# Four chained image blocks on one core: attention on 32-row tiles of TensorE in two sets of four banks, and a token-major third residual and tail

## What is computed

```
L0: x1 = x + wp.attention(q, k, v of groupnorm(x))                   one head, 256 x 256 scores
L1: pam = x1 + g1 * attention(16-channel q, k; 128-channel v)
    x2  = pam + g2 * softmax(max - pam.pam^T).pam                    attention between channels
L2: q, k = [x2 ; emb] @ Wq, Wk (8 heads of 16),  v = x2 @ Wv
    x3  = x2 + Wout.concat_h softmax(q_h.k_h^T / 4).v_h + bout       16 score matrices of 256 x 256 in all
L3: f = chan_ln(x3);  q, k, v = depthwise3x3(conv1x1(f))
    q = softmax over each head's 16 channels, k = softmax over the pixels
    o = silu(q.(k^T v));   x4 = x3 + chan_ln(out_w.o)
    out = x4 + ff_w2.chan_ln(gelu(ff_w1.chan_ln(x4)))
```

## Time and profile before

| | |
|---|---|
| median of 3 runs | 92.72 us (92.59 to 92.74) |
| the profiled execution | 93.64 us, of which the span is 91.8 us |
| mean granted TensorE clock in it | 0.981 |
| PE / PEld busy | 81.8 us / 60.2 us |
| DVE / ACT / POOL busy | 66.5 / 53.1 / 30.8 us |
| chain that ended last | PE 53%, DVE 20%, ACT 10%, issue 6%, POOL 6%, DMA 3% |

### The profile page before, as it was taken

The page is one execution under the profiler, slowest core; times in us unless marked ns, Lnnn a source line. Parts: engine busy times, 40 slices in busy tenths (PEclk is TensorE's granted clock), DMA queues, the critical chain, the costliest instruction groups (busy, mean ns, idle before and its releaser), DMA issues.

```text
span 91.8 us, 1634 instructions
## 1 busy us (share of the span) xinstructions
PE 81.8 (89%) x507; PEld 60.2 (66%) x510; DVE 66.5 (72%) x195; ACT 53.1 (58%) x168; POOL 30.8 (34%) x62
## 2 busy tenths in 40 slices
PE   4987997999998899899999998999999768979960
PEld 1246875576966588688676865689899535655640
DVE  1537878663685777978795998797999964887860
ACT  4002393546433118999899997992497646803830
POOL 7430598000000079400010002087876820326320
PEclk9999999995699999999999999999999999999999
DMA  1999200000000003929700000000000000000003
GB/s 28 239 323 405 115 0 0 0 7 0 0 0 4 0 0 105 286 70 255 208 0 0 0 0 0 7 0 0 0 0 4 0 0 11 0 0 4 0 3 111
DMA packets 5561, 5.01 MB, mean 55 GB/s; under 512 B 304, under 2 KB 5040, under 8 KB 5552
## 3 DMA queue, kind: packets, MB, share of 16 engines
q1 hardware_dynamic: 5408, 4.77, 16.9%
q10 hardware_dynamic: 144, 0.13, 0.4%
HBM read 3.59 MB, written 1.31 MB: 53 GB/s over the span
## 4 chain that ended last, share of the span: by engine, by line
PE 53%; DVE 20%; ACT 10%; issue 6%; POOL 6%; DMA 3%; POOLq 0%; DVEq 0%; ACTq 0%
PE bank L886 8%; PE bank L1068 6%; POOL vacc L279 4%; PE bank L1087 3%; ACT p L401 3%; PE bank L879 3%; DVE st L507 3%; DMA x<-in_x 3%; DVE nmax L700 2%; PE bank L1005 2%; PE bank L982 2%; PE bank L1148 2%; PE bank L1035 2%; PE bank L927 2%; DVE mv L511 2%
## 5 line engine op out<-in xcount | busy, mean ns | idle before, releaser
L368 ACT ACTIVATE p<-bank,nmax 128x256 f32<-128x256 f32 x32 | 14.9, 485 | 1.2 <-DVE nmax L700 1.0
L886 PE MATMUL bank<-wa,p 128*128 128x128 f32 x80 | 13.4, 290 | 0.3 <-ACT pT L375 0.3
L279 POOL TENSOR_TENSOR vacc<-vacc,p 128x240 f32<-128x240 f32 (+1 forms) x16 | 10.8, 674 | 6.8 <-ACT p L401 5.1
L700 DVE TENSOR_REDUCE nmax<-bank 128x2 f32<-128x512 f32 x16 | 10.7, 680 | 2.6 <-PE bank L1068 2.6
L886 PEld LDWEIGHTS bank<-wa,p 128*128 128x128 f32 x80 | 10.0, 149 | 2.9 <-issue 0.9
L239 POOL TENSOR_TENSOR rs<-ve,mhalf 128x2 f32<-128x2 f32 x8 | 5.6, 694 | 17.7 <-DVE ve L514 17.7
L259 POOL TENSOR_SCALAR qh<-q,wb 128x256 f32<-128x256 f32 x8 | 4.5, 587 | 17.1 <-DVE q L687 17.1
L894 PE MATMUL bank<-warm 128*128 128x512 bf16 x25 | 8.3, 446 | 1.3 <-DVE warm L520 1.2
L1148 PE MATMUL bank<-convw,fsh 128*128 128x128 f32 x72 | 9.0, 275 | 0.0
L1148 PEld LDWEIGHTS bank<-convw,fsh 128*128 128x128 f32 x72 | 8.7, 192 | 0.2
L1068 PE MATMUL bank<-k,qh 128*128 128x256 f32 x32 | 8.2, 383 | 0.4 <-ACT p L368 0.4
(11 more groups left out here) (204 smaller groups left out, 174.8 us busy)
## 6 DMA issues: line engine op xcount, KB each, us to landing
wc<-in_pack_c SPq DMA_DIRECT2D x1, 649.0 KB, 7.4
wb<-in_pack_b SPq DMA_DIRECT2D x1, 612.0 KB, 6.3
tapw<-in_taps SPq DMA_DIRECT2D x1, 576.0 KB, 8.2
stack_q<-stacks_q SPq DMA_DIRECT2D x2, 256.0 KB, 3.6
stack_k<-stacks_k SPq DMA_DIRECT2D x2, 256.0 KB, 4.0
stacks_q<-parts_q SPq DMA_DIRECT2D x2, 192.0 KB, 2.3
stacks_k<-parts_k SPq DMA_DIRECT2D x2, 192.0 KB, 2.7
wa<-in_pack_a SPq DMA_DIRECT2D x1, 320.0 KB, 3.9
```

The lines of the kernel that those rows point to most:

```text
L279: nc.gpsimd.tensor_add(vacc[b][:, oy, ox], vacc[b][:, oy, ox], vprod[n - 1][:, iy, ix]).then_inc(s["vsum_d"], 1)
L368: nc.scalar.activation(p2[u % P2_RING][:, t, :], tiles(bank[u % S2_BANKS])[:, t, :], ACT.Exp, bias=nmax2[b][:, h, t:t + 1], accum_out=sum2 ...
L700: nc.vector.tensor_reduce(nmax2[b][:, h, :], tiles(bank[u % S2_BANKS]), AX.X, ALU.max, negate=True).then_inc(s["max2_d"], 1)
L886: last = nc.tensor.transpose(tiles(dst)[:, i, t * 128:(t + 1) * 128], src[:, t, i * 128:(i + 1) * 128], ident)
```

## The change

What it does:

- **L1**: `q1` and `k1` get 128 rows (POOL sets them to zero first), so that the scores use all rows. A product `wg_mean` (384 columns) and one `keep_clock` product go ahead of `qk1_product`. DVE subtracts that mean from the 1x1 weights (`wgc`), which takes the centring out of L3. The embedding is multiplied straight into the banks of q and k (`embedding(n)`), which then accumulate.
- **L2**: a group is four heads of one batch. q and k are masked into two halves (`qm2`, `km2`), so a head is 16 of 32 rows. `group_scores` makes four heads' scores as eight products on 32-row tiles, each head in a bank of its own (2, 3, 6, 7). `group_max` writes the negated maxima into columns of `nmx2`; PE transposes them (`max_transposes`); `shift_add` adds them to the queries as one more row, which meets a row of ones in `km2`. `group_scores_T` then makes the transposed, shifted scores in banks 0, 1, 4, 5, and one exp per head writes `pT2` directly. The values have columns of ones, so `group_mix` also gives the sums. The transposes and copies of the probabilities, the masking on POOL, the bf16 parts and their DRAM transfers are gone. New after the mix: ACT copies it out, PE transposes it, DVE divides, PE transposes back, and a copy gives `o2`.
- **L3**: `x3_tokens` makes x3 with tokens on partitions in PSUM; `f_scale` scales it by the inverse root, and a transpose and a copy give `f`. x4 and y are also token-major, transposed on the way in and out. The spreads over partitions are gone. A second product with `outwg` (out_w with its gain) feeds x4.
- `vprod` has one buffer set per batch, and ACT no longer waits for the sums of batch 0.
- The lists of all engines in L3 are written anew. The two batches no longer go as a pair. Of the four `keep_clock` places in L3, one is left.

The core of the diff (bodies of functions, then the new orders):

```diff
-                nc.gpsimd.memset(v2[b][:, :, :], 0.0).then_inc(s["v2_zeroed"], 1)
+                nc.gpsimd.memset(v2[b][:, :, :], 1.0).then_inc(s["v2_set"], 1)
...
-        vprod = [p2[n // NT][:, n % NT, :].rearrange("p (h w) -> p h w", h=H) for n in range(TAPS - 1)]
+        vprod = [per_batch(f"vprod_{n}", [128, H, W]) for n in range(TAPS - 1)]
...
+            def group_scores(grp):
+                b, g = divmod(grp, NG)
+                pe.wait_ge(s["q2_d"], NG * b + g + 1)
+                pe.wait_ge(s["k2_d"], NG * b + g + 1)
+                for t in range(NT):
+                    for i in range(HG):
+                        rows = slice(QUAD * i, QUAD * (i + 1))
+                        product = nc.tensor.matmul(tiles(bank[SCORE_BANKS[i]])[:, t, :], qm2[b][rows, g, t * 128:(t + 1) * 128],
+                                                   km2[b][rows, g, :], start=True, stop=True, tile_position=(QUAD * i, 0))
...
+            def group_max(grp):
...
+                for i in range(HG):
+                    u = grp * HG + i
+                    dve.wait_ge(s["s2_p"], u + 1)
+                    col = QUAD * i + SHIFT_ROW[g]
+                    nc.vector.tensor_reduce(nmx2[g][:, :, col:col + 1], tiles(bank[SCORE_BANKS[i]]), AX.X, ALU.max,
+                                            negate=True).then_inc(s["max2_d"], 1)
...
+            def shift_add(grp):
+                b, g = divmod(grp, NG)
+                dve.wait_ge(s["nT2_p"], grp + 1)
+                nc.vector.tensor_add(qa2[b][:, g, :], bank[SHIFT_BANK[grp]][:, 0:N], qm2[b][:, g, :]).then_inc(s["qa2_d"], 1)
...
+            def head_exp(u):
+                act.wait_ge(s["st2_p"], u + 1)
+                if u >= PT2_RING:
+                    act.wait_ge(s["pv2_p"], (u - PT2_RING) // HG + 1)
+                nc.scalar.activation(pT2[u % PT2_RING][:, :, :], tiles(bank[SCORE_T_BANKS[u % HG]]), ACT.Exp).then_inc(s["e2_d"], 1)
...
+            def x3_tokens(b):
+                pe.wait_ge((s["o2_d"], s["o2b_d"])[b], 1)
+                pe.wait_ge(s["xb2_d"], b + 1)
+                for t in range(NT):
+                    cols = slice(t * 128, (t + 1) * 128)
+                    nc.tensor.matmul(LA[b][:, t * C:(t + 1) * C], xb2[b][:, cols], ident, start=True, stop=False)
+                    last = nc.tensor.matmul(LA[b][:, t * C:(t + 1) * C], o2[b][:, cols], B("wout"), start=False, stop=True)
...
+            def f_scale(b):
+                act.wait_ge(s["rs3_d"], b + 1)
+                for t in range(NT):
+                    nc.scalar.activation(fT[b][:, t, :], tiles(LA[b], 4)[:, t, :], ACT.Copy, scale=rs3[b][:, 0, t:t + 1]).then_inc(s["fT_d"], 1)
...
POOL, L3
-                             (root4, 0), (root4, 1), (root5, 0), (root5, 1), (root6, 0), (root6, 1)):
+            for stage, b in ((root3, 0), (v_sums(1, 4), 0), (root3, 1), (v_sums(4, TAPS), 0), (v_sums(1, 6), 1), (root4, 0),
+                             (v_sums(6, TAPS), 1), (root5, 0), (root4, 1), (root6, 0), (root5, 1), (root6, 1)):
...
ACT, from the products of batch 1 on
+                             (v_products(3, TAPS), 1), (ekT_evac, 0), (qT_evac, 0), (v3_evac, 0),
+                             (k_exp, 1), (o3_tanh, 0), (q_exp, 1), (gelu_table, 1), (ekT_evac, 1), (x4_evac, 0), (qT_evac, 1), (v3_evac, 1),
+                             (o3_tanh, 1), (gelu, 0), (hT_evac, 0), (x4_evac, 1), (gelu, 1), (y_evac, 0), (hT_evac, 1), (y_evac, 1)):
...
DVE, L3
+            for stage, b in ((k_taps_0, 0), (x3_stats, 1), (k_taps_3, 0), (k_taps_6, 0), (k_taps_8, 0), (k_taps_0, 1), (q_max, 0), (k_sums, 0),
+                             (k_taps_3, 1), (q_norm, 0), (k_taps_6, 1), (context, 0), (k_taps_8, 1), (q_max, 1), (silu, 0), (q_norm, 1),
+                             (y_stats, 0), (k_sums, 1), (x4_sum, 0), (x4_stats, 0), (context, 1), (silu, 1), (h_stats, 0), (y_stats, 1),
+                             (y_sum, 0), (x4_sum, 1), (x4_stats, 1), (h_stats, 1), (y_sum, 1)):
```

More of the change, by code:

```diff
@@ L480, in _, with y_evac @@
[L480 to L485 removed]
+            def y_evac(b):
+                act.wait_ge(s["yt_p"], b + 1)
+                nc.scalar.activation(y[b][:, :], LB[b][:, 0:N], ACT.Copy).then_inc(s["y_d"], 1)
@@ L866, in _ @@
[L866 to L871 removed]
+                dve.wait_ge(s["rs6_d"], b + 1)
@@ new lines, in y_sum @@
+                for t in range(NT):
+                    nc.vector.scalar_tensor_tensor(yT[b][:, t, :], tiles(LA[b], 4)[:, t, :], rs3[b][:, 3, t:t + 1], x4T[b][:, t, :],
+                                                   ALU.mult, ALU.add).then_inc(s["yT_d"], 1)
+            q2_evac(0)
+            group_max(0)
+            q2_evac(1)
+            shift_add(0)
+            group_max(1)
+            shift_add(1)
+            group_max(2)
+            shift_add(2)
+            group_max(3)
+            shift_add(3)
@@ new lines, in max_transposes, with group_scores_T @@
+            def max_transposes(grp):
+                pe.wait_ge(s["max2_d"], HG * (grp + 1))
+                for t in range(NT):
+                    last = nc.tensor.transpose(bank[SHIFT_BANK[grp]][:, t * 128:(t + 1) * 128], nmx2[grp % NG][:, t, :], ident)
+                last.then_inc(s["nT2_p"], 1)
+            def group_scores_T(grp):
+                b, g = divmod(grp, NG)
+                pe.wait_ge(s["qa2_d"], grp + 1)
+                for t in range(NT):
+                    for i in range(HG):
+                        rows = slice(QUAD * i, QUAD * (i + 1))
+                        product = nc.tensor.matmul(tiles(bank[SCORE_T_BANKS[i]])[:, t, :], km2[b][rows, g, t * 128:(t + 1) * 128],
+                                                   qa2[b][rows, g, :], start=True, stop=True, tile_position=(QUAD * i, 0))
+                        if t == NT - 1:
+                            product.then_inc(s["st2_p"], 1)
@@ L1209, in h_products @@
                 pe.wait_ge(s["w1c_w"], 1)
-                for t in range(NT):
-                    last = nc.tensor.transpose(LA[b][:, t * C:(t + 1) * C], x4[b][:, t * 128:(t + 1) * 128], ident)
-                last.then_inc(s["x4T_p"], 1)
                 for t in range(NT):
@@ new lines, in ff_product, with y_transposes @@
+                last.then_inc(s["ff_p"], 1)
+            def y_transposes(b):
+                for t in range(NT):
+                    pe.wait_ge(s["yT_d"], NT * b + t + 1)
+                    last = nc.tensor.transpose(LB[b][:, t * 128:(t + 1) * 128], yT[b][:, t, :], ident)
+                last.then_inc(s["yt_p"], 1)
+            pe.wait_ge(s["x2_d"], NB)
+            pe.wait_ge(s["outwg_w"], 1)
+            group_scores(0)
+            qk2(1)
+            v2_product(0)
+            v2_product(1)
```

559 lines of the change are left out of this document (248 added, 311 removed).

## The result

The changed kernel takes 103.8 us (median of 4 runs, 103.08 to 104.38) beside 92.73 for the kernel before (4 runs): a ratio of 1.117, interval 1.107 to 1.127. I had forecast 97.8, at most 102.0. The direction was right and the size was not: 11.1 us more, where I had 5.1.

A forecast was written before the change was run, and what follows sets the result against it. ACT paced batch 1's attention, POOL's sums the stretch to 74.23, then both batches in step. Terms -1.84 - 0.17 + 0.26 + 6.94 - 0.68 = +4.51, with the clock +5.1, gave 97.8 us; range 91.5 to 102.

The forecast's parts named there:

- Term 1: Start to the first transpose of pam (L1): -1.84 us, from the embedding leaving and the clock staying up.
- Term 2: First transpose of pam to L2's first row maximum: -0.17 us, masks and waits against removed POOL masking.
- Term 3: Attention, first maximum to batch 0's first k tap: +0.26 us, with four 32-row tiles fully overlapping and period 4.03.
- Rival (a): Attention tiles do not run side by side: 102 us with queued loads, 110 with no overlap; chance 0.09.
- Term 4: First k tap to transposes of batch 1's sums: +6.94 us, as POOL's last three sums wait behind batch 0's root4.
- (b): POOL isn't held, so batch 1's sums are transposed up to 6.6 us earlier: 90.6 us; chance 0.24.
- (c): New order costs half of term 4 (3.5): 94.3 us; chance 0.63 together with the forecast.
- (d): It doesn't matter: terms cancel within 0.2%; chance 0.04.
- term 5: Transposes of batch 1's sums to the last y: -0.68 us, spreads gone but waits for batch 0 taking most back.
- term 6: Clock likely falls in the tail where PE is nearly empty: +0.6 us (0 to 3.6).

The follow-up runs named there:

- b1_no_keep: The kernel before without its ten idle products in L3; 92.54 us beside 92.62, ratio 1.000.
- e9_split: Changed kernel with L3 lists reordered, idle products, batch 1's last k tap earlier, and later groups' scores issued in two halves; 95.29 us, ratio 1.027.
- e10_silu: e9_split with batch 1's silu ahead of batch 0's x4 statistics on DVE; 94.56 us, ratio 1.018.
- b2_no_emb: The kernel before without the embedding's products in L1, qe2 and ke2 set to zero; 91.75 us beside 92.47, ratio 0.991.
- e3_keep: Changed kernel with 36 idle products in PE's waits from batch 0's context to the end, in place of three; 100.6 us, ratio 1.088.
- e2_order: Changed kernel with L3's lists rewritten on all engines so both batches' tails go in step, same instructions; 96.87 us, ratio 1.047.
- e5_keep_all: Changed kernel with e2_order's lists plus idle products in L3 and in the attention's waits; 95.76 us, ratio 1.038.

## Why the prediction was wrong, and where it was right

**What bounds the kernel.** Right in kind. The clock's fall in L1 was the weak place: the profiled execution of before had one, and I took it for the kernel's. Of the 17 runs of it that were taken beside `b1_no_keep`, `e9_split` and `e10_silu`, 13 had a clock of 0.998 or more and four had 0.981 and took 0.9 us longer.

**Term 1, -1.84: measured -0.08 in undisturbed runs.** The text itself says "if the timed runs have no fall before either, it is 0.9"; the sum took the other value and then subtracted 0.92 for the median on top. So 0.9 of the 1.84 was counted twice: once as a fall that the change would end, and once as the distance to the median, whose runs have no fall. The rest is the embedding, which was worth 0.7 and not 1.45 (`b2_no_emb`; the 1.45 is a reading at the low clock), and `wg_mean` with the keep product, behind which `qk1_product` starts at 16.61 where `b1_no_keep` has 16.22. PE then transposes p earlier (20.91, not 21.60), but waits for the row sums of the exps until 22.37, where `b1_no_keep` has them at 22.09. That 32 rows brought the clock down in L1 is not shown by anything here: before keeps 1.00 in most runs with the same rows.

**Term 2, -0.17: measured +0.11.** Within what small waits do.

**Term 3, +0.26: measured +1.14.** The period is 4.23 and not 4.03. From the last maximum to the transposes it is 0.15, where I had 0.06, and from the start of L1052 to the first maximum 1.26, where I had 1.17. Three periods make 0.6. The way from the last maximum to the first tap is 8.85, not 8.55 (which the sum used; the walk ends at 8.58). Full overlap holds: 16 passes on four tiles in 1.15, which is 0.374 for the last, 0.104 for the first one's load and 0.224 for each of a tile's three steps from pass to pass, near L982's 0.216. The Trainium skill (TensorE: Matmul & The Clock Gate, Part 3) says that a load overlaps running products only in another row group. By that each step would be 0.32 by my estimate, as every tile's loads go to its own row group. The trace of the change, with 0.224, disagrees with it as the earlier trace rows did. Rival (a) is out.

**Term 4, +6.94: measured +6.88.** The walk held to a few tenths: root3(1) ends 13.2 after the last maximum (I had 13.05), the wait ahead of root4(0) is 6.60 us (5.9), its root starts at 28.5 (28.1) and PE takes the sums at 31.5 (31.25). Undoing the order alone brings 6.9 us of time. That the two numbers differ by only 0.06 is in part luck: 0.36 us of the 6.88 is the low clock from 76 us on, which the walk did not have. With the clock up (`e3_keep`) the stretch is 22.26, and the term +6.52. Rivals (b), (c) and (d) are out.

**Terms 5 and 6, -0.08 together: measured +3.35. This is the step that failed, term 6 above all.** I wrote that a fall was likely and that at 1.2 GHz eight stages would cost 3.6 us in all; then I took 0.6, because the one fall in the trace of before was short. `e3_keep`, with 36 idle products in the waits, gives the size: 3.3 us in this piece, 3.2 in the time. So term 6 should have stood near its upper end of 3.6. The reason that I had for 3.6 was the right kind, product stages at half speed, but not the same stages. Two falls, of 10 and of about 3 us, take some 8 of the 21 us of this piece. In them are not eight stages of batch 1 but four (the transposes of its sums, context, o3 and h) and, in front of o3, h of batch 0. The fall in the earlier trace rows ended while PE was busy, 4.00 of 4.00 us. In the tail PE is busy 7.39 of the 10 us and the clock stays down. Without the clock, term 5 is 0.0 (17.63 beside 17.62 to the end of the span) and not -0.68, so 0.7 us of the miss here is term 5's and the rest the clock's: two batches out of step have no gain from the spreads that went.

**How the parts add up.** From the forecast's +5.1 to 11.4 in the profiles: 1.8 (term 1), 0.3 (term 2), 0.9 (term 3), -0.1 (term 4), 3.4 (terms 5 and 6). The order and the clock are not two independent costs. The clock is worth 3.2 us in the order of the changed kernel, and 1.1 (`e2_order` to `e5_keep_all`) once the batches go in step. In the same way the order is worth 6.9 us where the clock falls (103.8 to 96.87), and 4.8 where idle products hold it up in both (100.6 to 95.76). In the profiles of that second pair term 4's stretch gets 6.7 shorter, 22.26 to 15.54, but the piece after the transposes gets longer, from 17.63 to 19.9, since batch 0's tail is no longer done before it. Putting the order right takes 6.9, the idle products 1.1, two more steps on DVE 1.2 and 0.9; 1.0 us remains, where the attention of the new form is 1.1 us longer.

**What stays open.** What brought the clock back at 86 and kept it down until then isn't settled: PE was as busy before 86 as after 88. Nor is it settled when a nearly empty PE loses the clock: from 40 to 42 us it is busy 0.56 of 2 us in the changed kernel and 0.76 in `e1_pool`, and only in the second does the clock fall, to 0.50 from 42 to 44. A pairing of the old attention with the new tail was not tried.

## What to carry to other kernels

Walk the lists of the new order to the first place where an instruction waits for a slow chain, and count what is queued behind it on that engine; this walk gave 6.94 for 6.88 (6.52 with the clock up). Then ask what PE still has to do during such a wait: where it has next to nothing, price the whole tail behind it at the lower clock, not one stage, and try idle products there before anything else. Take the base of a comparison from an execution at full clock, and where one cannot be had, do not count the end of its lapse as a gain, nor take a price from a row inside the lapse.

## What the runs showed that I had not expected

- The clock was down for 10 us on end in the tail (76 to 86, granted 0.50) while PE was busy 7.39 of them; the fall that I had seen before lasted 3.4.
- The kernel before has a clock of 0.997 or more in most runs with its ten idle products in L3 (13 of 17) and without them (8 of 10), at 92.62 and 92.54 us: they do nothing for its time.
- Two 32-row tiles take as long as four: 8 records in 1.13 us, 16 in 1.15.
- A row maximum of two tiles over 128 columns each comes 0.34 us after the one before it, over 256 columns each 0.60.
